# Attention into routed experts: eight stores of zeros spread over the last iteration, and one set of small loads issued ahead of the first expert's weights

## The reference, cut to what matters

```python
xn = _layernorm(x)
attn = softmax(mask(relu(xn @ Wq + bq) @ relu(xn @ Wk + bk).T / sqrt(16)))   # 16 heads, causal
a = gamma * normalise(attn @ relu(xn @ Wv + bv) + xn) + beta
rw, sel = top_k(xn @ router_w.T + experts_bias, 2)          # two experts a token, of 8
f = sum over the two of softmax(rw) * (silu(xn @ w1[e]) * (xn @ w3[e])) @ w2[e]
s = (silu(xn @ sw1) * (xn @ sw3)) @ sw2
out = x + a + f + s
```

## Time and profile before

| | |
|---|---|
| three times | 1890.43, 1895.26, 1896.06 us; median 1895.26 |
| the profiled execution's own time | 1895.93 us |
| its span on the core | 1894.2 us |
| attention phase | 0 to 942 us of the span |
| busy: TensorE, weight loads, VectorE, ScalarE, GpSimd | 1724.7, 1293.7, 1274.0, 1090.4, 1173.4 us |
| iterations 14 and 15, about | 834 to 894 us and 894 to 938 us |

### The profile page before, as it was taken

The page is one execution under the profiler, slowest core; times in us unless marked ns, Lnnn a source line. Parts: engine busy times, 40 slices in busy tenths (PEclk is TensorE's granted clock), DMA queues, the critical chain, the costliest instruction groups (busy, mean ns, idle before and its releaser), DMA issues.

```text
span 1894.2 us, 35895 instructions
## 1 busy us (share of the span) xinstructions
PE 1724.7 (91%) x12070; PEld 1293.7 (68%) x12070; DVE 1274.0 (67%) x3089; ACT 1090.4 (58%) x2066; POOL 1173.4 (62%) x1435
## 2 busy tenths in 40 slices
PE   3589999989999999987699999999999998999998
PEld 2345555555555555544388888888888888788887
DVE  6788898888888888867175544544544544466666
ACT  5247666666676666645456666666666675233332
POOL 3465557777777677723467777677677684544443
PEclk9689999999999999988799999999999999999999
DMA  1544344554555445444366667657667664454443
GB/s 53 151 124 136 109 147 147 169 169 138 157 162 166 137 143 166 150 158 160 129 198 209 206 193 233 194 193 232 193 195 231 193 227 145 135 156 145 149 155 99
DMA packets 244224, 310.30 MB, mean 164 GB/s; under 512 B 31466, under 2 KB 209268, under 8 KB 237940
## 3 DMA queue, kind: packets, MB, share of 16 engines
q1 hardware_dynamic: 231796, 274.98, 45.6%
q0 software_dynamic: 12288, 33.57, 5.5%
HBM read 209.60 MB, written 98.34 MB: 163 GB/s over the span
## 4 chain that ended last, share of the span: by engine, by line
PE 43%; ACT 3%; DVE 2%; DMA 1%; POOL 1%; another core or an unknown queue 1%; issue 0%; SPq 0%; DVEq 0%; ACTq 0%
PE gu L1960 27%; PE yp L1974 14%; PE xt L1949 2%; DVE hf L1820 1%; ACT hid_h L1727 1%; DVE passed L1864 1%; ACT sil L1725 0%; ACT w_up_h L1719 0%; DMA w_raw<-in_L_ffn_w_dram 0%; DVE hid_l L1823 0%; DMA w_raw<-in_L_ffn_sw_dram 0%; DVE xc L1831 0%; ACT junk L1784 0%; ACT xc L1733 0%
## 5 line engine op out<-in xcount | busy, mean ns | idle before, releaser
L656 ACT ACTIVATE pT<-st_ps 128x512 f32<-128x512 f32 x682 | 369.0, 562 | 285.1 <-PE st_ps L1266 242.7
L926 DVE CUSTOM_DVE_ANT_0 s_ps<-s_ps,masks 128x384 f32<-128x384 f32 (+1 forms) x512 | 315.0, 632 | 46.8 <-PE s_ps L1245 39.3
L1960 PE MATMUL gu<-xc,w_up_h 128*128 128x512 f32 (+1 forms) x1120 | 339.0, 386 | 6.0 <-DVE hf L1820 4.7
L1820 DVE TENSOR_TENSOR hf<-sil,gu 128x512 f32<-128x512 f32 (+1 forms) x220 | 143.8, 654 | 265.3 <-ACT sil L1725 259.8
L1245 PE MATMUL s_ps<-k_aug,q_aug 97*128 97x512 bf16 (+3 forms) x1024 | 265.5, 312 | 42.8 <-DVE mx L926 15.9
L1264 PE MATMUL st_ps<-q_aug,k_aug 99*128 99x512 bf16 (+1 forms) x992 | 273.3, 308 | 19.0 <-ACT pT L656 10.9
L1823 DVE TENSOR_TENSOR hid_l<-hf,hid_h 128x512 fp32r<-128x512 f32 (+1 forms) x220 | 168.4, 766 | 147.6 <-ACT hid_h L1727 135.7
L1960 PEld LDWEIGHTS gu<-xc,w_up_h 128*128 128x128 f32 x1120 | 205.2, 190 | 51.6 <-issue 6.1
L1727 ACT ACTIVATE hid_h<-hf 128x512 fp32r<-128x512 f32 (+1 forms) x220 | 133.1, 605 | 181.2 <-DVE hf L1820 176.3
L1725 ACT ACTIVATE sil<-gu 128x512 f32<-128x512 f32 (+1 forms) x220 | 123.9, 563 | 194.7 <-PE gu L1960 177.9
L1635 POOL DMA_INDIRECT got<-expert_results,place x128 | 122.8, 959 | 166.1 <-DVE hf L1820 141.3
(11 more groups left out here) (259 smaller groups left out, 4041.7 us busy)
## 6 DMA issues: line engine op xcount, KB each, us to landing
early_raw<-in_L_ffn_w_dram SPq DMA_DIRECT2D x60, 512.0 KB
w_raw<-in_L_ffn_w_dram SPq DMA_DIRECT2D x57, 512.0 KB, 5.6
part_scr<-parts SPq DMA_DIRECT2D x64, 384.0 KB
q_aug<-part_scr SPq DMA_DIRECT2D x192, 128.0 KB
k_aug<-part_scr SPq DMA_DIRECT2D x192, 128.0 KB
early_raw<-expert_rows SPq DMA_DIRECT2D x34, 512.0 KB
expert_results<-yo SPq DMA_DIRECT2D x32, 512.0 KB, 3.3
x_sb<-in_L_attn_x_dram SPq DMA_DIRECT2D x16, 512.0 KB, 4.4
```

Of the source, the lines that this page charges most:

```text
L656: fn(pT[j][:, h:h + heads], unit_view(column_bank(b, u), heads, w), ACT.Exp).then_inc(exp_done, 1)
L926: vec.tensor_tensor_reduce(bank[:, 0:keys], bank[:, 0:keys], masks[:, 2 * C + P - keys:2 * C + P], 1.0, LOWEST, ALU.add, ALU.max, mx[:, h ...
L1820: vec.tensor_tensor(hf[:, m % 2, 0:w], sil[:, m % 2, 0:w], gu[m % 2][:, 1, 0:w], ALU.mult).then_inc(h_done, 1)
L1960: last = mm(gu[m % 2][:, a, 0:width(n)], w_up[wpar][x][:, a, c, P * m:P * (m + 1)], xc[par][:, y, c, 0:width(n)], start=k == 0, stop=k == ...
```

## The change

`fill_ends` is no longer called twice, for experts 0 to 3 in iteration 14 and for 4 to 7 in iteration 15. It is called once, in iteration 15, for all eight, and waits before each for `st_scored`: the scores of unit 4 for expert 0, of unit 8 for expert 1, up to unit 32 for expert 7. In every iteration `load_neg(i + 1, ..., 0)` now stands ahead of `if i == B - 2: load_early()`. That moves something in iteration 14 alone, where the small loads came behind the weights and four stores of zeros, and now come ahead of the weights.

```diff
+        FILL_EVERY = 4
...
-            def fill_ends(experts):
+            def fill_ends(b):
 
                 await_(sp, table_ready, 1)
-                for e in experts:
+                for e in range(E):
+                    await_(sp, st_scored, NU * b + FILL_EVERY * (e + 1))
                     sp.reg_load(end_reg, carry_i[0:1, e:e + 1])
                     end = sp.snap(end_reg)
                     sp.dma_start(expert_rows[bass.ds(end, S), :].rearrange("(t p) c -> p t c", p=P), zeros.to_broadcast([P, NT, C])
...
+                if maxima:
+                    load_neg(i + 1, 1 - par, 0)
                 if i == B - 2:
                     load_early()
-                    fill_ends(range(E // 2))
-                if maxima:
-                    load_neg(i + 1, 1 - par, 0)
                 for b in scattered_in(i + 1)[:2]:
                     fetch(b)
                 if i == B - 1:
-                    fill_ends(range(E // 2, E))
+                    fill_ends(i)
```

## The result

The changed kernel takes 1899.64 us (median of 10 runs, 1897.36 to 1904.8), the kernel before 1893.82 us (10 runs, 1890.43 to 1896.06). The ratio is 1.0032, with a 95% interval of 1.0024 to 1.0040: 5.8 us or 0.3% slower. The profiled execution took 1901.0 us, its span is 1899.3 us. The ratios of this document leave out one slow execution of 2760.61 us, among ten of the kernel that is named "low pieces first" further down.

A forecast was written before the change was run, and what follows sets the result against it. No engine is full; rings between TensorE, ScalarE and VectorE set the time. Terms 3.6 + 0 + 0 + 0 = +3.6 us on the median 1895.26 gave 1898.9 us; range 1889.5 to 1903.5 with two in ten left out.

The forecast's parts named there:

- The weights come later: Iteration 14: early weights, issued behind the maxima copies, land at 887.0; ScalarE waits 3.6 us, bounds 1.3 and 6.5.
- The whole wait counts: End of iteration 14: ScalarE is busy nearly all the time behind its wait, so all of it counts, +3.6 us.
- The stores of iteration 14 and 15: Moving the stores of zeros leaves the stalls as they were: 0; bounds 0 to 1.90 us gained, and -4.28 to +4.28.
- the rival that the burst makes the stalls: Iterations 14 and 15: bursts of stores make the stalls, so thinning them is faster, 1892.7 or 1888.9 us; chance 0.20.
- The end: Behind iteration 15: the later last store and first chunk's load stay hidden, landing by 941.2 before TensorE's need at 941.94; 0.
- The spread stores: Iteration 15: five stores among GpSimd's scatters turn the third `weigh` from 2.32 to 6.60 us; +7.9, 1903.2 us; chance 0.14.

The follow-up runs named there:

- low pieces first: Kernel before with GpSimd's six low pieces of the early weights ahead of the scatters of iteration 15 instead of behind them; ratio 1.0002.
- the order alone: Kernel before with only the copies of the negated maxima issued ahead of the early weights in iteration 14, stores of zeros left four and four; ratio 1.0030.
- ScalarE asking later: Changed kernel with ScalarE's six pieces of the early weights moved from units 33 to 42 to units 38 to 43 of iteration 14; ratio 1.0002.
- The stores alone: Changed kernel with the weights again ahead of the copies of the maxima, so only the stores of zeros are moved; ratio 1.0007 to the kernel before.
- stores or scatters last: Two variants of the kernel before: all eight stores of zeros in iteration 16, 1898.28 us; iteration 15's scatters held until its last exponential, 1901.27 us.
- breaking the run: Kernel before with GpSimd's six low pieces placed singly behind scatter pairs 2 to 7 of iteration 15; 1883.45 us, ratio 0.9953.
- the kernel that only holds the scatters back: Kernel before with the scatters of iteration 15 released only from its 24th exponential on, low pieces left behind them; ratio 1.0033.

## Why the prediction came out as it did

The direction, the place and the mechanism were right; the time forecast was 1898.9 us and the measured one is 1899.64. That the two are so near is in part luck. The forecast stood on a median of three times, 1895.26, and the median of ten is 1893.82, 1.4 us lower. The difference from before was forecast at 3.6 us and is 5.8 by the medians: the one term of the sum was sized too small, and the base made up for a part of it. The text set 0.3% as its bound for no change and gave 0.68 to that side of it and 0.22 to slower. The ratio of 1.0032 lies just beyond that bound, with an interval that reaches to both sides; against its own 1900.9 us, the measured time lies just inside. So neither side can be called met.

*The weights come later: right, undersized.* 3.6 us were forecast and 4.49 + 0.65 measured. All of iteration 14 was 1.6 us later in this execution; against the forecast moved by that much, SyncE began the copies of the maxima at 875.22 (forecast 873.6 + 1.6 = 875.2). They took 5.80 us and not 4.95. That price was taken from a place where the queue was quieter (DMA share 0.10 there, 0.26 here), but the same eight copies at the same place took 4.94 us both with the order alone and with ScalarE asking later, so the excess differs from one execution to the next. Reading the register took 1.0 us, and 1.2 in those two, and not 0.80. The first weight was issued at 882.03, 1.1 us later than 880.9. From there the forecast held: the slowest of the three took 6.2 us, where 6.7 was taken (with the order alone it was 7.3). That it was right to take the slowest of three landings for the last, and not the middle one, shows: with 5.1 us the wait would have been 1.1 us shorter. The rule of the Trainium skill that the prediction set beside it ("DMA: Bandwidth & Descriptors", section "Anatomy of one DMA — SWDGE (gpsimd) path"), 2.0 us and the bytes over 436 GB/s, gave an estimate of 5.6 us from the first issue for all three. ScalarE took the first piece 7.5 us behind that issue. The rule is a fit for transfers issued by GpSimd, and these are SyncE's; here the rows and not the rule had the size.

*The whole wait counts: right, and a little more.* From the first piece to the end of iteration 14 are 0.65 us more than before, and the prediction had no term for that. It goes with a clock that stayed at 0.50 until about 896, where it was at 1.00 from 888 on in the kernel before.

*The stores of iteration 14 and 15, 0: right within what the runs can tell.* The stores alone measure 1.0007, whose interval (0.9998 to 1.0015) holds no change and a loss of up to 3 us. The gaps of the changed kernel are 3.97, 6.55 and 3.82 + 3.02 us, where 4.2, 6.6 and 6.1 were forecast. The choice against the rival that the burst makes the stalls was argued from the low DMA share beside the second one; the kernels with stores or scatters last showed it.

*The end, 0: right.* The first chunk's load was issued at 935.61, released by the last store, 11.8 us later than before (6.7 of them because everything was), and the store of y came at 944.69 behind it, as soon as VectorE had written y (944.66).

*The rivals.* The faster one fell: without any store the stalls are 5.17 and 5.65 us. The spread stores added no third stall: the third `weigh` is 2.32 us. Its argument, that stalls lie in runs of scatters, was the right half of it, and I did not follow it to its own price, which was larger than that of the change: 8.4 us for breaking the run.

What stays open is by which way a run of scatters holds TensorE and ScalarE. The rows say "remote" and "issue", which names nothing. That it is not the number of scatters is shown: with the same 16, iteration 15 and the way to the barrier are 9.5 us shorter when a piece of other work lies between most of the pairs. Whether the length of the unbroken run counts, or how closely scatters follow one another inside it, the runs don't separate.

## What to carry to other kernels

A transfer's place in an in-order queue is worth what its consumer lacks: before one is moved behind a wait, compare its new landing with the time when the consumer asks, and take the slowest landing of the group if the consumer waits for all of it. The copies that were moved ahead were ten microseconds early, and the weights that were moved back had less to spare than the 10 to 13 us they were moved by.

Look at the idle time itself as well as at the gap behind one instruction: in two kernels here the gap fell to 2.3 us and the stall stood one unit later. When an engine stalls with no releaser named, line up the stalls with the long runs of every other engine, and not only with the transfers under suspicion. Putting GpSimd's computing between its indirect transfers cost nothing and gave 0.5%, or 8.4 us; the most that the prediction had priced for the change was 6.4.

## What the runs showed of the hardware

Unbroken runs of indirect scatters by GpSimd (128 KB each, one every 1.27 us) hold up TensorE and ScalarE. With six and eight in a row, ScalarE stood 5.28 us twice; with sixteen it stood 4.90 and 10.68 us, and went on 1.2 us behind the end of the last one (0.5 us in the kernel that only holds the scatters back). In pairs with 1.27 us of other work between them there was no such stall (gaps of 2.32 us, and 3.65 beside the four that were left in a row). A high DMA share does not explain it: it was 0.29 in a stretch that holds more than half of the second stall. How the scatters hold the other engines is not known. Four stores of 512 KB in the same iteration without any scatter beside them made none (the kernel with the scatters last).
